# Making L2's table of transformed rows inside the message pass that gathers from it

## The reference

```
V = weight.reshape(in_dim, num_bases, out_dim)
W_rel = jnp.matmul(w_comp, V).reshape(num_rels, in_dim, out_dim)      # 90 relations, 16 x 16 each
h_src = h[src]
e = jnp.concatenate([h_src @ Ws.T, he @ Ws.T, h[dst] @ Ws.T], axis=1) @ Wa.T
msg = jnp.einsum('ei,eio->eo', h_src, W_rel[rel_type]) * e
h_out = jax.ops.segment_sum(msg, dst, num_segments=n_nodes)
```

## Time and profile before

| | us |
|---|---|
| median of 3 runs | 8562.17 |
| lowest, highest | 8555.83, 8563.68 |
| the profiled execution, its own time | 8550.26 |
| its span in the profile | 8548.6 |

### The profile page before, as it was taken

How to read it: one execution, slowest core, us unless ns; L and a number is a source line. 1 busy time by engine, 2 the same in 40 slices (tenths; PEclk the granted TensorE clock), 3 DMA queues, 4 the chain that set the end, 5 groups by cost and what they waited for, 6 DMA issues and landing times. The chain is left out here.

```text
span 8548.6 us, 233535 instructions
## 1 busy us (share of the span) xinstructions
PE 6428.4 (75%) x55142; PEld 5292.3 (62%) x55143; DVE 4918.4 (58%) x13561; ACT 2820.3 (33%) x8471; POOL 5192.9 (61%) x7408
## 2 busy tenths in 40 slices
PE   1222215767699998999899989997866666888998
PEld 1111113555477776888688868886455555887998
DVE  7333345867455655666466646664322223998999
ACT  1222212545333333333333333332133333222554
POOL 2777754756477766777577757774277775222554
PEclk8555556555599999999999999998555555999999
DMA  2000003434388886888688878885200001332232
GB/s 66 3 3 3 3 29 104 120 97 120 88 221 216 216 197 181 222 221 222 161 222 222 222 164 223 222 222 121 95 7 7 7 7 24 82 82 57 73 73 59
DMA packets 1319112, 1000.54 MB, mean 117 GB/s; under 512 B 479354, under 2 KB 1223183, under 8 KB 1318092
## 3 DMA queue, kind: packets, MB, share of 16 engines
q1 hardware_dynamic: 941322, 649.30, 27.7%
q0 software_dynamic: 134272, 178.98, 10.8%
q10 hardware_dynamic: 243392, 170.76, 6.9%
HBM read 951.88 MB, written 54.19 MB: 118 GB/s over the span
## 5 line engine op out<-in xcount | busy, mean ns | idle before, releaser
L1480 POOL DMA_INDIRECT qg<-q_tab,qidx x2520 | 2389.2, 948 | 940.1 <-issue 699.2
L1635 DVE COPY ps<-b 128x384 f32<-128x384 f32 x1120 | 628.0, 561 | 1381.2 <-ACT h L1600 1374.8
L1067 PE MATMUL ps<-rhs_i,ohi 128*128 128x128 f32 (+2 forms) x8640 | 1215.7, 266 | 210.1 <-issue 197.2
L1067 PEld LDWEIGHTS ps<-rhs_i,ohi 128*128 128x128 f32 (+1 forms) x8640 | 1000.4, 163 | 342.5 <-issue 282.0
L1033 POOL COPY near<-x 128x48 bf16 x2160 | 675.9, 351 | 789.4 <-PE ps L1056 434.0
L1195 POOL DMA_INDIRECT got_m<-y_tab,idx_m x832 | 815.8, 981 | 478.8 <-issue 251.4
L1549 PE MATMUL ps<-ohm,h 128*128 128x128 f32 x6720 | 1032.9, 290 | 65.3 <-DVE ps L1635 33.9
L1549 PEld LDWEIGHTS ps<-ohm,h 128*128 128x128 f32 x6720 | 838.8, 192 | 257.7 <-issue 242.8
L1593 ACT ACTIVATE h<-ps,b 128x384 f32<-128x384 f32 x1120 | 650.2, 581 | 1052.2 <-PE ps L1531 955.6
L375 POOL DMA_INDIRECT list_by_src<-ring,rpos x808 | 783.1, 969 | 349.0 <-issue 255.0
L1212 PE MATMUL ps<-rhs_m,ohi_m 128*128 x2880 | 668.1, 403 | 416.1 <-ACT rhs_m L1238 387.3
(11 more groups left out here) (442 smaller groups left out, 8623.6 us busy)
## 6 DMA issues: line engine op xcount, KB each, us to landing
pb<-p_tab ACTq DMA_DIRECT2D x1680, 96.0 KB
pb<-p_tab SPq DMA_DIRECT2D x1680, 96.0 KB
places<-place_by_turn SPq DMA_DIRECT2D x560, 192.0 KB
places_i<-place_by_meeting SPq DMA_DIRECT2D x360, 256.0 KB, 3.4
places_i<-place_by_meeting SPq DMA_DIRECT2D x720, 128.0 KB, 3.1
qb<-q_tab SPq DMA_DIRECT2D x840, 64.0 KB
qg<-q_tab,qidx POOLq DMA_INDIRECT x2520
nears<-near_by_turn SPq DMA_DIRECT2D x560, 64.0 KB
```

What stands on the lines that cost most here:

```text
L1067: m = pe.matmul(ps[:, bass.ds(to[j], width)], ohi[:, h, j, :], rhs[:, h, j, 0:width], start=False, stop=True, skip_group_check=True)
L1480: pool.indirect_dma_start(qg[:, h, j, :], None, q_tab, IndirectOffsetOnAxis(ap=qidx[:, h, j:j + 1], axis=0)).then_inc(m_got[h], 16)
```

## The change

- `message_pass` gets `xT`, `wr` and `yb`, and makes the table itself. On TensorE the 75 products come after the two blanking products and ahead of the first sum; on VectorE the 75 copies come ahead of the first `ohi_m`. The products use PSUM banks 2 to 7. The program block that made the table is gone.
- SP, after sending block b, waits for the landing of block b - 1 and adds one to `y_ready`.
- ScalarE reads, for each of the first 32 gather groups (`KY` = 8 rounds of four, written out), the block of the group's last tile from `blk_at` into a register and waits for `y_ready` to reach that block plus one before it writes `idx_m`. Later groups wait for all 25 blocks.
- The blocks of the tiles are kept for this: VectorE writes `blk_i` behind `blk_s`, SP stores it as `tile_block`, and the message pass loads its first 128 numbers.
- `y_tab` is blanked during the scatter: VectorE sets `blank` (128 x 1530) as its first work there, and SP sends it 25 times, waiting for each landing.
- `wr` is loaded straight to its place; `wl` and its copy are gone.

```diff
@@ the scatter's program block
+                @block.sync
+                def _(sp):
+                    sp.wait_ge(blank_set, 1)
+                    for b in range(NB):
+                        sp.dma_start(y_tab[b * P * NREL:(b + 1) * P * NREL, :].rearrange("(p r) o -> p (r o)", p=P), blank[:, :]).then_inc(blank_out, 16)
+                        sp.wait_ge(blank_out, 16 * (b + 1))
+
                 @block.vector
                 def _(dve):
+                    dve.memset(blank[:, :], 0.0).then_inc(blank_set, 1)
                     v_chain(dve, dve.memset(upto[:, 0:1], 0.0))
@@ the tiles' blocks
+                    sp.wait_ge(b_blk, 1)
+                    sp.dma_start(tile_block[:, :], blk_i[:, :]).then_inc(b_out, 16)
                     sp.wait_ge(b_plc, 3)
...
                     v_chain(dve, dve.tensor_scalar(blk_s[0:1, :], blkt[0:1, :], float(P), None, ALU.mult))
+                    dve.tensor_scalar(blk_i[0:1, :], blkt[0:1, :], float(NB - 1), None, ALU.min).then_inc(b_blk, 1)
@@ message_pass: SP
+                        sp.dma_start(blk_at[:, :], tile_block[:, 0:KY * U * G]).then_inc(d_blk, 16)
                         sp.dma_start(at_m[:, :], meet_l2[0:NGI, :].rearrange("(a n) k -> a (n k)", a=1)).then_inc(d_at, 16)
+
+                        def landed(b):
+                            sp.wait_ge(y_out[b % 2], 16 * (b // 2 + 1))
+                            sp.sem_inc(y_ready, 1)
+
+                        for b in range(NB):
+                            sp.wait_ge(to_pe.sem, b_cp + 3 * b + 3)
+                            sp.dma_start(y_tab[b * P * NREL:(b + 1) * P * NREL, :].rearrange("(p r) o -> p (r o)", p=P),
+                                         yb[:, b % 2, :]).then_inc(y_out[b % 2], 16)
+                            if b >= 1:
+                                landed(b - 1)
+                        landed(NB - 1)
@@ message_pass: TensorE
                         for i in range(2):
                             pe.matmul(banks[i], nothing[:, 0:P], nothing[:, :], start=True, stop=True)
+                        for b in range(NB):
+                            for c in range(3):
+                                n = 3 * b + c
+                                if n >= 6:
+                                    pe.wait_ge(to_pe.sem, b_cp + n - 5)
+                                pe.matmul(y_bank(n), xT[:, b * P:(b + 1) * P],
+                                          wr[:, :, :].rearrange("i r o -> i (r o)")[:, c * YC:(c + 1) * YC], start=True, stop=True).then_inc(from_pe.sem, 1)
                         pe.wait_ge(d_at, 16)
@@ message_pass: ScalarE
+                            if not isinstance(k, int) or k >= KY:
+                                act.wait_ge(y_ready, NB)
+                            else:
+                                last = (k * U + h) * G + G - 1
+                                of = address(mybir.EngineType.Activation, blk_at[0:1, last:last + 1], NB - 1)
+                                act.wait_ge(y_ready, (of[0] & 31) + 1)
                             act.activation(idx[:, h, :], rel_s[:, bass.ds((k * U + h) * G, G)], ACT.Copy).then_inc(d_idx, 1)
@@ message_pass: VectorE
+                        for b in range(NB):
+                            if b >= 2:
+                                dve.wait_ge(y_out[b % 2], 16 * (b // 2))
+                            for c in range(3):
+                                n = 3 * b + c
+                                dve.wait_ge(from_pe.sem, b_mm + n + 1)
+                                dve.tensor_copy(yb[:, b % 2, c * YC:(c + 1) * YC], y_bank(n)).then_inc(to_pe.sem, 1)
+
                         def build(k, h):
@@ L2, ahead of it
-                load([(wl[:, :, :], g_tab.rearrange("(r i o) -> i r o", r=NREL, i=16))])
+                load([(wr[:, :, 0:16], g_tab.rearrange("(r i o) -> i r o", r=NREL, i=16))])
...
-                        v_chain(dve, dve.tensor_copy(wr[:, :, 0:16], wl[:, :, :]))
...
-            message_pass()
+                message_pass(xT, wr, yb)
```

More of the change, by code:

```diff
@@ L108, in gnn_kernel @@
         meet_l2 = dram("meet_l2", [NIP // G, 2 * G], I32)
+        tile_block = dram("tile_block", [1, NT], I32)
         p_tab = dram("p_tab", [NP, 3 * HID], BF16)
@@ L343, in gnn_kernel @@
             identb = sb("identb", [P, P], BF16, st)
+            blank = sb("blank", [P, NREL * 17], F32, st)
+            blank_set, blank_out = sem("blank_set"), sem("blank_out")
             ring = sb("ring", [P, 2, 2 * J, W], F32, st)
@@ L593, in gnn_kernel @@
             blk_s = sb("blk_s", [1, NT], F32, st)
+            blk_i = sb("blk_i", [1, NT], I32, st)
+            b_blk = sem("b_blk")
             iv = sb("iv", [P, IC], F32, st)
@@ L643, in _ @@
                     sp.dma_start(meet_l2.rearrange("(p g) k -> p g k", p=P), l2_i[:, :, :]).then_inc(b_out, 16)
+                    sp.wait_ge(b_blk, 1)
+                    sp.dma_start(tile_block[:, :], blk_i[:, :]).then_inc(b_out, 16)
                     sp.wait_ge(b_plc, 3)
                     sp.dma_start(place_i[0, :].rearrange("(c i p) -> i c p", c=12, p=P), place_buf[0:IQ, :, :]).then_inc(b_out, 16)
-                    sp.wait_ge(b_out, 16 * 3)
+                    sp.wait_ge(b_out, 16 * 4)
                 @block.tensor
@@ L1167, in gnn_kernel, with message_pass, y_bank @@
         d_got = [sem(f"d_got{h}") for h in range(U)]
-        def message_pass():
+        y_ready, d_blk = sem("y_ready"), sem("d_blk")
+        KY = 8
+        def message_pass(xT, wr, yb):
+            b_mm, b_cp = from_pe.base(NB * 3), to_pe.base(NB * 3)
+            YC = NREL * 17 // 3
+            y_out = [sem("y_out0"), sem("y_out1")]
+            def y_bank(n):
+                return banks[2 + n % 6][:, 0:YC]
             with ExitStack() as st:
+                blk_at = sb("blk_at", [1, KY * U * G], I32, st)
                 idx = sb("idx_m", [P, U, G], I32, st)
@@ L1240, in step @@
                             m.then_inc(d_rhs, 1)
+                        act.wait_ge(d_blk, 16)
                         for h in range(U - 1):
                             indices(0, h)
-                        turns(act, step)
+                        for k in range(KY):
+                            for h in range(U):
+                                step(k, h)
+                        with act.Fori(KY, K - 1) as k:
+                            for h in range(U):
+                                step(k, h)
+                        for h in range(U):
+                            step(K - 1, h)
                     @block.vector
                     def _(dve):
+                        for b in range(NB):
[5 more added lines that the diff above has]
+                                dve.tensor_copy(yb[:, b % 2, c * YC:(c + 1) * YC], y_bank(n)).then_inc(to_pe.sem, 1)
                         def build(k, h):
@@ L1914, in gnn_kernel @@
                 yb = sb("yb", [P, 2, NREL * 17], F32, sy)
-                wl = sb("wl", [FIN, NREL, 16], F32, sy)
                 xT = sb("xT2", [FIN, NP], F32, sy)
-                y_out = [sem("y_out0"), sem("y_out1")]
                 load([(wcT[:, :], a["L2_gnn_w_comp"].rearrange("r b -> b r")),
@@ L1929, in gnn_kernel @@
                 save([(g_tab.rearrange("(i r o) -> r i o", i=16, r=NREL), gg[:, :, :])])
-                load([(wl[:, :, :], g_tab.rearrange("(r i o) -> i r o", r=NREL, i=16))])
+                load([(wr[:, :, 0:16], g_tab.rearrange("(r i o) -> i r o", r=NREL, i=16))])
                 turn_block(x, FIN, xT)
-                b_mm, b_cp = from_pe.base(NB * 3), to_pe.base(NB * 3)
                 with nc.Block() as block:
```

## The result

| | before | changed |
|---|---|---|
| median, us | 8562.92 (4 runs) | 8446.01 (4 runs) |
| lowest, highest | 8555.83, 8571.49 | 8430.1, 8451.42 |
| the profiled execution (span) | 8550.26 (8548.6) | 8430.1 (8428.4) |

The ratio is 0.986, interval 0.9843 to 0.9877: 105 to 134 us faster. Predicted were 8470, range 8438 to 8486.

What follows compares the result with a forecast made beforehand. GpSimd's issue of gathers, behind the table, was taken to bound the message pass. Last gather 93.3 us earlier (120.6 less 27 given back) and +1.4 for the memset sum to -91.9, so 8470.3 us; range 8438 to 8486.

Steps and rivals of the forecast that it cites:

- First gather: Start of the message pass: the first gather waits only for block 0 and comes 120.6 us earlier.
- While the table is made: Message pass beside the table's products: no y_ready wait but the first, no hold by VectorE's copies, gathers every 1.25 us.
- C: Rival: VectorE's table copies hold gathers as ohi_m does, step 1.70 us; last gather 70.5 us earlier, 8493 us; chance 6%.
- Catching up: Message pass behind the table: 38 waiting sum groups take 117 us, 67.2 gathers held at 1.74 us; 27 us given back.
- it is soon caught and then stays: Within the backlog: a gather falls into step with VectorE's ohi_m and is held every 1.74 us throughout.
- B: Rival: gathers not held for long, mean step stays 1.285 us through the backlog; last gather 123.9 us earlier, 8440 us; 8%.
- The stage: Message pass from the table to the last gather: last gather 93.3 us earlier in all.
- A: Rival: TensorE's clock rises while it catches up, backlog 42 us; last gather 112.9 us earlier, 8451 us; chance 12%.
- Front: Start of the scatter: VectorE's memset of blank comes first and adds 1.4 us.
- E: Rival: slow blanking transfers drag through the scatter; at 13 us a landing 160 us lost, 8630 us; chance 3%.
- D: Rival: register wait or block order lets no gather go before all blocks land; first gather 6117.8, 8564 us; chance 3%.

Runs made afterwards that it cites:

- whole table: The changed kernel with every gather group's idx_m waiting for all 25 blocks; 10480.57 us on a slower chip, 0.9996 of the kernel before.
- kernel before with PSUM: The kernel before with only the row of numbers that ohi_m compares against read from PSUM; 10530.25 us, 1.0032 of the kernel before.
- front only: The kernel before plus only the blanking in the scatter and the tiles' blocks; 10506.46 and 10515.38 us on two slower chips, 1.0017 and 1.0018.
- written-out kernel: The changed kernel with all groups of ScalarE's message-pass part written out with constant addresses; 8451.9 us, 0.9874 of the kernel before.

## Why the prediction was right, and where it was off

**First gather.** Predicted 120.6 us closer to the table's start; 133.4 became 12.8, so 120.6. The trace shows this directly; on a slower chip, the run with the whole table shows that the gain goes when the early gather does.

**While the table is made.** No wait for `y_ready` but the first, no gather held by VectorE's copies from PSUM: the step is 1.25 us, also beside a copy that starts 0.01 us ahead of the gather (5981.66 and 5981.67 above, 0.94 us). Of the two bounds the value taken, nothing, was right; C is out.

**Catching up: the term that was mis-sized.** Predicted were 67 gathers of 1.74 us in 117 us, and 27 us given back. Measured: TensorE is busy from its first sum (6097.1) to about 6240, 143 us. From 6113 it has 560 records in 127 us, that is 70 sum groups of 1.81 us. GpSimd starts 86 gathers there, one every 1.48 us (its idle time, 127 - 100.8 = 26.2 us at 0.30 each, says 87 of 1.46). So the stretch is longer and the loss in it smaller; given back were 16.7 us. Put into the prediction's own formula, 1.81 us a sum group and 1.47 us a gather make its 38 waiting groups last about 147 us, an estimate that fits the measured 143. The failing step is "it is soon caught and then stays": it is caught, but at each turn of TensorE's loop, every four sum groups, the step of `ohi_m` is 2.12 us instead of 1.74, and that lets GpSimd go. Two rows in step at one place were carried over a whole stretch; the longer step was in the same trace (`ohi_m` at 6991.11 and 6993.22, and 39 such steps in all) and was not looked for. B, an undisturbed mean of 1.285 us through the backlog, was wrong on the other side: from the table's first product to the last gather it has 1077.7 us, the forecast 1108.3, and 1097.5 were measured.

**The stage:** from the first product to the last gather 1201.5 us became 1097.5, so 104.0 less, where 93.3 was predicted; the difference of 10.7 is the catching up.

**Clock.** 0.50 through the table and the backlog: A is out. The Trainium skill, "TensorE: Matmul & The Clock Gate", "Why this matters for your kernels", would have had the upper level there; this trace does not agree, with 97 to 98% busy for well over 100 us in each of two stretches.

**Front.** +1.9 us at the scatter's start, predicted +1.4: the memset is 1.33 us, with the gap behind it. The scatter did not become longer, so E is out, as is D. Its landings stayed at 2.1, but that tells nothing of transfers side by side: the prediction had each blanking transfer take 4.5 us and the two overlap for 22 us, while they took 3.6 each and were over at 183.7, before the scatter's first. What a landing beside the blanking would take, no run shows.

**What no term covered.** -104.0 and the front's 3.1 (where L0 begins, `near` at 1413.8 before and 1416.9 after) make -101, the profiled executions differ by 120.2 and the medians by 117. The missing part lies in L1, which the change doesn't touch: from its first gather to the table's first product 3630.9 us before, 3609.5, 3619.7 and 3615.8 in the three profiles with the change on the faster chips (the expectations speak of 14 us, by these rows it is 21.3), and the clock granted in it is not the same (from 4050 to 4200 a mean of 0.86 before, 0.91 after). On the slower chips it went the other way: 5051.9 in the kernel before with PSUM, 5070.0 to 5077.5 in six others on the first two of those chips and 5055.3 in the run with the whole table, and there front only was 0.17 and 0.18% slower. So L1 alone moves by 10 to 25 us between kernels that have the same rows in it, as much as the forecast was off. Why it moves was not found; one profile of the kernel before can't tell a kernel's own share from that of an execution. Its share, 16 us by the medians and 19 by the profiles, put the median under the predicted 8470 more than the catching up did (10.7).

**How much of the hit was luck.** The measured 8446.0 lies below the range that the prediction gave its forecast by itself, 8456 to 8486. It lies inside the stated 8438 to 8486 only because that was widened for A and B, and neither came true. The mechanism of the main term, the first gather, was right to within 0.1 us; that the total fell inside the range was in part luck.

## What to carry to other kernels

A stage that only waits for all of a table can start with the first block, and the gain is close to the whole length of the table if the consumer's own step sets the pass: here 104.0 of 120.6 us. What is late next (here the sums) costs no wait as long as its input is kept for the whole pass, though its engines can still slow the others, here by 16.7 us in held gathers. Before costing a stretch by two engines in step, look for what breaks the step, a loop turn or a block border, and price the mean. Where GpSimd issues transfers beside VectorE, one operand of VectorE's instruction moved to PSUM can be worth about half as much as such a reordering: 60 us in the written-out kernel, an estimated 47.5 us in the changed one, and no gain where another engine ends the pass.

## What the runs showed of the chip that was not expected

- On three of the four chips of these runs the same program took 22 to 24% longer. There TensorE and ScalarE, and VectorE too, stand still between rows with nothing shown that they wait for: in gaps of 5 us and more, and in steps of 1.40 us. It meets rows with addresses from registers and rows with constant ones, so addresses from registers are not its condition. What causes it, the chip or something beside it, stays open: the run meant to tell fell on a chip without it.
- Which engine ends a stage depends on that: gathers at 8446 us, sums at 10405 us, for one and the same kernel. Moving the iota to PSUM, worth 60 us on the faster chip, cost 34 and 39 us on two of the others and nothing clear of noise on the third (9 us). Why it cost anything, and not nothing, was not found.
